# A two-layer mixture-of-experts kernel on one core: first layer's slots split behind three blocks, hidden units on partitions, GpSimd clears ahead of stores

## The chip, the cores and the metric

One Trainium2 chip (trn2), one core. The metric is the device time in microseconds of one launch; the median of 3 runs is 466.99 us (463.61 to 469.23).

## The reference

Shapes: `x` is (32, 128, 128), that is 4096 tokens of 128 values. Two layers, each a residual:

```python
def _L0_cond_ref(x, y, w, coeffs):             # polynomial in side input, condition and x
    X = jnp.stack([jnp.ones_like(x), x, x * x], axis=1)
    ...
    dW = jnp.einsum('abc,kaj,kbi,kcij->kij', coeffs, X, Y, Wp)
def _L0_ffn_ref(x, Wg, bg, W1, b1, W2, b2):     # 8 experts, 2 per token, hidden 256
    logits = jnp.einsum('bsd,de->bse', x, Wg) + bg
    ...
    h = jax.nn.gelu(jnp.einsum('bsd,edh->besh', x, W1) + b1[None, :, None, :], approximate=False)
    out = jnp.einsum('besh,ehd->besd', h, W2) + b2[None, :, None, :]
    y = jnp.einsum('bse,besd->bsd', gates, out)
def _L1_cond_ref(x, h0, Wx, Wh, b):             # recurrence over the 128 positions
    ...
        next_h = jnp.tanh(xp_t + prev_h @ Wh)
def _L1_ffn_ref(...):                           # layer norm, router, shared expert, 8 experts, 2 per token
    out = _swiglu(xf, sWg, sWu, sWd)
    for e in range(NUM_EXPERTS):
        out = out + w[:, e:e + 1] * _swiglu(xf, Wg[e], Wu[e], Wd[e])
x = x + _L0_ffn_ref(_L0_cond_ref(fside_BxS_0, cond_1024, x, L0_cond_coeffs), ...)
x = x + _L1_ffn_ref(_L1_cond_ref(x, cond_1024, L1_cond_Wx, L1_cond_Wh, L1_cond_b), ...)
```

## The kernel before

The program is written by engine: one function for each of SyncE (SP), GpSimd (POOL), ScalarE (ACT), VectorE (DVE) and TensorE (PE), each executed in the order in which it is written, held together by semaphores. The 4096 tokens are cut into 8 blocks of 512 (16 positions of 32 sequences). Each layer sorts its tokens by expert through DRAM: a GpSimd indirect DMA sends the 128 rows of one tile and one choice into `regions` (`send`), SyncE loads 128 rows of one expert back at a time, which is one slot, and after the expert a second indirect DMA (`send_result`) stores the slot's 128 result rows into `results`, in the order of the tokens. 8192 choices need 64 slots, and up to 7 more for the experts' ragged ends: 71 per layer.

Stages, in order of time:

- First part. Blocks in groups (0), (1, 2), (3, 4), (5, 6), (7): transposes, the polynomial, the router (`choose`, `gates`, `positions`). GpSimd runs `scatter0(g)`: 64 sends, each behind `rest()`, a memset of a tile and a wait for it. `copy_z` of a group waits until the group two earlier is sent, since the rows' buffers are a ring of two.
- First layer's slots, `slots0` on PE, ACT and DVE: for slot j the rows are transposed, copied by ACT (`copy_turned0`), multiplied with W1 (`hidden_slot`: tokens on the partitions of the result, 256 columns), DVE adds the bias (`add_bias`), ACT takes the gelu, PE transposes twice (`turn_act`), ACT copies (`copy_act`), PE multiplies with W2 (`slot_down`), DVE adds the bias and multiplies with the gate (`gate_result`), and GpSimd stores. `SLOTS` splits the slots in two parts, each with a table that says which expert and which rows a slot takes: the first part (`FULL_SLOTS`) needs only the sends of the groups up to `CUT`, the second all of them. `DONE` says how many stores must have landed before the blocks up to the cut can be read back (`parts`). The results' ring `y_row` has 24 places, so DVE can be 24 slots ahead of GpSimd.
- Recurrent bodies, `stream_body(i, i % 2)` for i = 0 to 7: the 16 steps of block i, one PE matmul and one ACT tanh each, and between them the work of other blocks, placed by tables of step numbers (`PAIR_AT`, `DOWN_AT`, `LOGIT1_AT`, `XP_AT`, ...): layer norm, router and shared expert of block i - 1, the sum x1 of block i + 1 (`add_one`, `sum_x1`, `turn_back`). GpSimd's part of a body is `inv_std(n)` (the inverse standard deviation that `logits1(n)` on DVE waits for) and `scatter1(m)`.
- Second layer's slots, `slots1`: 4 slots of the last block's shared expert, then 71 of the experts. On GpSimd the eight sends of block 6 stand ahead of the layer's store 0, and the eight of block 7 one each ahead of stores 8 to 15 (`SCATTER_AT`).
- End: `load_parts` reads the results back, `add_parts` sums, the output is written.

GpSimd's program in a row: the factors, `scatter0` of five groups, 71 `send_result(0, r)`, then in a loop `inv_std(i - 1)` and the sends that are due, then 71 `send_result(1, r)`. `inv_std(0)` so stands behind the first layer's last store:

```python
            for r in range(LAYER_SLOTS[0]):
                send_result(0, r)
            m = 0
            for i in range(1, NB):
                inv_std(i - 1)
                while m < SPLIT * NT * TOPK and scatter_step(m) < STEPS * (i + 1) + VAR_STEP:
                    scatter1(m)
                    m += 1
```

In a body DVE works through `positions`, `variance1`, `add_shared`, `sum_x1`, `multiply(i - 1, 0)`, `logits1`, `choose`, `multiply(i - 1, 1)`, `gates`; PE's `down1` of a half c waits for `multiply(i - 1, c)`, and what stands behind `down1` on PE, the next step of the recurrence too, waits with it.

## Time and profile before

| what | us |
|---|---|
| median of 3 runs | 466.99 (463.61 to 469.23) |
| profiled execution, device time | 464.02 |
| its span, first to last instruction | 462.2 |
| TensorE busy, share of the span | 398.0 (86%) |
| VectorE busy | 339.4 (73%) |
| GpSimd busy | 307.9 (67%) |
| ScalarE busy | 206.6 (45%) |

The profiled execution's device time is 1.8 us above its span. A row of the timeline gives start, duration, engine, line, operation, output<-input, count, and in brackets how long the engine had been idle before and what released it. Names are those of the tensors; buffer numbers are left out. "issue" is idle time for which the profile shows no releaser.

### The profile page before, as it was taken

The page shows a single profiled execution, that of the slowest core. Times are in us where ns is not written, and L with a number is a line of the kernel's source. Part 1 is how long each engine was busy: PE and PEld are TensorE (multiplying, and loading weights), DVE is VectorE, ACT ScalarE, POOL GpSimd, SP SyncE. Part 2 cuts the span into 40 slices and gives each one's busy share as a digit, 9 for nine tenths or more (in the row PEclk, how much of TensorE's full clock was granted, in tenths as well). Part 3 has the DMA queues.
Part 4 walks back from the last instruction along what each step waited for, and adds up shares of the span by engine and source line. Part 5 has one row for each costly group of instructions (what it writes and reads, how often), then busy time and mean ns, then how long its engine had stood idle before and what let it go on. Part 6 is the DMA issues. An engine that isn't in the chain of part 4 may idle for free.

```text
span 462.2 us, 10225 instructions
## 1 busy us (share of the span) xinstructions
PE 398.0 (86%) x2428; PEld 324.8 (70%) x2428; DVE 339.4 (73%) x1299; ACT 206.6 (45%) x660; POOL 307.9 (67%) x369
## 2 busy tenths in 40 slices
PE   3888868366999999999999999997985999999950
PEld 3475635354799999976778888775774888888840
DVE  4788885538788888885767776878689566677782
ACT  1121204040677777754554554553442455555520
POOL 0548888888877777777346666665645777676670
PEclk9898785557799999999999999999898899999985
DMA  5996111113454444263311111112421353333756
GB/s 147 276 328 198 41 42 40 40 44 96 111 145 113 106 116 108 78 193 128 109 63 42 42 42 36 41 42 72 105 62 54 87 136 104 99 94 83 276 159 210
DMA packets 48150, 49.79 MB, mean 108 GB/s; under 512 B 8627, under 2 KB 37246, under 8 KB 47966
## 3 DMA queue, kind: packets, MB, share of 16 engines
q1 hardware_dynamic: 38680, 30.46, 24.5%
q0 software_dynamic: 8640, 17.84, 11.6%
q10 hardware_dynamic: 774, 0.84, 0.6%
q8 instruction: 23, 0.38, 0.3%
q14 instruction: 33, 0.27, 0.2%
HBM read 27.99 MB, written 21.12 MB: 106 GB/s over the span
## 4 chain that ended last, share of the span: by engine, by line
PE 60%; DVE 13%; POOL 12%; issue 6%; DMA 5%; ACT 1%; SPq 1%; DVEq 0%; POOLq 0%; ACTq 0%
PE banks L1271 49%; POOL regions L519 9%; PE banks L1275 8%; PE banks L1360 3%; POOL pause L509 3%; DMA parts<-results 3%; DMA results<-y_row,y_dest 1%; DMA base<-in_x 1%; POOL results L553 1%; DVE y_row L1053 1%; DVE act_row L1151 1%; DVE state_lo L1144 1%; DMA regions<-parts,pos 1%; ACT wgu_hi L617 0%; DVE blocks L978 0%
## 5 line engine op out<-in xcount | busy, mean ns | idle before, releaser
L553 POOL DMA_INDIRECT results<-y_row,y_dest x142 | 138.1, 973 | 56.9 <-issue 33.2
L519 POOL DMA_INDIRECT regions<-first_w,pos x64 | 62.9, 983 | 45.9 <-ACT hT L654 30.6
L519 POOL DMA_INDIRECT regions<-parts,pos x64 | 65.0, 1016 | 18.0 <-POOL pause L509 18.0
L654 ACT ACTIVATE hT<-banks,pcol 128x32 f32<-128x32 f32 x128 | 36.9, 288 | 52.9 <-PE banks L1271 52.3
L636 ACT COPY act_col<-banks 128x256 f32<-128x256 f32 x146 | 54.0, 370 | 11.0 <-PE banks L1275 10.1
L713 ACT ACTIVATE silu_row<-banks 128x256 f32<-128x256 f32 x75 | 28.8, 384 | 63.8 <-PE banks L1271 63.1
L1275 PE MATMUL banks<-const_sb,act_row 128*128 128x128 f32 x292 | 56.8, 277 | 0.0
L1271 PEld LDWEIGHTS banks<-hT,wh 128*128 128x128 f32 x256 | 39.2, 188 | 23.3 <-ACT hT L654 19.9
L1275 PEld LDWEIGHTS banks<-const_sb,act_row 128*128 128x128 f32 x292 | 41.7, 143 | 18.3 <-issue 1.8
L1151 DVE TENSOR_TENSOR act_row<-silu_row,banks 128x256 f32<-128x256 f32 x75 | 31.4, 420 | 28.8 <-ACT silu_row L713 26.1
L1271 PE MATMUL banks<-hT,wh 128*128 128x32 f32 x256 | 50.3, 279 | 0.0
L1271 PE MATMUL banks<-first_w,state 128*128 x142 | 44.7, 398 | 1.7 <-DVE silu_row L1038 1.4
L1271 PE MATMUL banks<-wd,act_col 128*128 x284 | 44.4, 280 | 1.0 <-DVE y_row L1053 0.9
L1271 PE MATMUL banks<-first_w,act_col 128*128 x284 | 43.7, 276 | 0.5 <-ACT act_col L636 0.3
L1271 PEld LDWEIGHTS banks<-wd,act_col 128*128 128x128 f32 x284 | 38.0, 195 | 1.4 <-issue 1.3
L1271 PEld LDWEIGHTS banks<-first_w,act_col 128*128 128x128 f32 x284 | 37.3, 191 | 1.2 <-issue 1.2
L1271 PE MATMUL banks<-hT,sw_raw 128*128 128x256 f32 x112 | 38.0, 421 | 0.0
L630 ACT ACTIVATE act_row<-silu_row 128x256 f32<-128x256 f32 x71 | 29.6, 417 | 14.4 <-DVE silu_row L1038 12.0
L1271 PE MATMUL banks<-wgu_hi,state_hi 128*128 x71 | 35.0, 492 | 0.7 <-issue 0.3
L1038 DVE TENSOR_TENSOR silu_row<-banks,first_w 128x256 f32<-128x256 f32 x71 | 29.6, 418 | 5.7 <-issue 3.0
L1271 PE MATMUL banks<-parts,xpow 96*128 96x512 f32 x48 | 30.7, 792 | 0.4 <-DVE parts L790 0.4
L509 POOL MEMSET pause<- 128x256 f32 x80 | 26.0, 326 | 5.6 <-issue 5.5
(192 smaller groups left out, 855.1 us busy)
## 6 DMA issues: line engine op xcount, KB each, us to landing
parts<-results SPq DMA_DIRECT2D x16, 512.0 KB, 5.0
hT<-regions SPq DMA_DIRECT2D x71, 65.0 KB, 2.1
wgu<-regions SPq DMA_DIRECT2D x71, 65.0 KB, 1.9
results<-y_row,y_dest POOLq DMA_INDIRECT x142, 2.3
base<-in_x SPq DMA_DIRECT2D x12, 128.0 KB, 3.1
out<-base SPq DMA_DIRECT2D x20, 64.0 KB
regions<-const_sb SPq DMA_DIRECT2D x18, 65.0 KB
first_w<-in_L_ffn_W SPq DMA_DIRECT2D x1, 1024.0 KB, 8.1
```

Source lines behind the costliest of these rows:

```text
L509: pool.memset(pause[:, :], 0.0).then_inc(rested, 1)
L519: pool.indirect_dma_start(regions[layer], bass.IndirectOffsetOnAxis(ap=poss[layer][q][:, t, k:k + 1], axis=0), hrows[layer][:, q, t, k, :] ...
L553: pool.indirect_dma_start(results[layer], bass.IndirectOffsetOnAxis(ap=y_dest[:, s:s + 1], axis=0), y_row[:, s, :], None).then_inc(results ...
L630: nc.scalar.activation(act_row[:, j % ACT_RING, :], silu_row[:, j % SILU_RING, :], ACT.Gelu).then_inc(slot_act[0], 1)
L636: nc.scalar.copy(act_col[:, j % ACT_RING, :], act_turned_ps[:, j % 2, 0:HID]).then_inc(act_copied[layer], 1)
L654: nc.scalar.activation(hT[:, hcols(n, step_col(s), B)], rnn_ps[:, p, step_col(s):step_col(s) + B], ACT.Tanh, bias=pcol[:, ROW_CB:ROW_CB + ...
L713: nc.scalar.activation(silu_row[:, q % SILU_RING, :], up_ps[:, q % 2, 0:HID], ACT.Silu).then_inc(slot_silu, 1)
L1038: dve.tensor_tensor(silu_row[:, j % SILU_RING, :], up_ps[:, j % 2, 0:HID], b1[:, bass.ds(e * HID, HID)], ALU.add).then_inc(biased, 1)
L1151: dve.tensor_tensor(act_row[:, q % ACT_RING, :], silu_row[:, q % SILU_RING, :], up_ps[:, q % 2, HID:2 * HID], ALU.mult).then_inc(slot_act[ ...
L1271: return nc.tensor.matmul(dst, w, v, start=start, stop=stop, **kw)
L1275: ins = nc.tensor.transpose(bank[:, t * P:(t + 1) * P], tile, ident)
L1360: nc.tensor.transpose(turned_ps[:, r % 2, 0:P], rows[layer][:, s, 0:D], ident).then_inc(turned[layer], 1)
```

## The change

- `CUT` goes from 2 to 1 and the first layer's first part from 32 slots to 16: it needs only the sends of blocks 0 to 2, the other 55 slots all of them. `DONE[0]` so goes from 47 stores to 31.
- The first expert's hidden units stand on the partitions: DVE copies a slot's W1 (128x256) into a ring (`copy_w1`), PE multiplies it, 128 columns at a time, with the transposed rows, ACT applies gelu with the bias from `pcol` by a column chosen in a register. `add_bias`, `turn_act` and `copy_act` are gone from the first layer; the last block's shared slots also lose their transposes and copies. Lags, rings and PSUM buffers are changed to suit.
- `rest()` clears 256 columns of `ypow` (96 partitions) in place of `pause` (128 partitions), and stands ahead of every `send_result` of both layers too. The sends of the bodies have none, as before, and lose a wait for the send before.
- In a body `down1`'s tiles are spread over steps 8, 9, 11, 12 and 14, 15, 15, 15; the ranks of the last blocks go from step 15 to 13; x1 of block 3 is made inside body 2, behind `multiply(1, 0)`.
- GpSimd's factors of block 2 wait for the first group's choice. The second part's table has temporaries of its own. The last sums are made by halves of a block. In body 7 `multiply_slot(0)` and `(1)` stand ahead of `gate_rows`.

```diff
-CUT = 2
-ALL_SLOTS, FULL_SLOTS = TOPK * TOK // P + E - 1, (32, 40)
+CUT = 1
+ALL_SLOTS, FULL_SLOTS = TOPK * TOK // P + E - 1, (16, 40)
...
-AHEAD, ACT_LAG, DOWN_LAG = 3, (3, 2), (5, 4)
-STATE_RING, SILU_RING, ACT_RING = 4, 3, 4
+AHEAD, ACT_LAG, DOWN_LAG = (4, 3), 2, (4, 3)
+STATE_RING, SILU_RING, ACT_RING, WEIGHT_RING, WEIGHTS_AHEAD = (6, 4), 3, (8, 4), 3, 2
+DEPTH = 3
...
-ROWS_AT, COPY_ROWS_AT, RANKS_AT, LAST_RANKS_AT = 0, (1, 2), 1, 15
-PAIR_AT, SILU_AT, DOWN_AT = (((2, 3), (5, 6)), ((8, 9), (11, 12))), (4, 10), ((13, 14), (15, 15))
+ROWS_AT, COPY_ROWS_AT, RANKS_AT, LAST_RANKS_AT = 0, (1, 2), 1, 13
+PAIR_AT, SILU_AT = (((2, 3), (5, 6)), ((8, 9), (11, 12))), (4, 10)
+DOWN_TILE_AT = (8, 9, 11, 12), (14, 15, 15, 15)
...
-SUM_AT = 61, 64, 67
+SUM_FROM = 60
+HALF_SUMS = -(-(ALL_SLOTS - SUM_FROM) // 4) * 4
...
             def rest():
 
                 rests[0] += 1
-                pool.memset(pause[:, :], 0.0).then_inc(rested, 1)
+                pool.memset(ypow[:, :, :], 0.0).then_inc(rested, 1)
                 pool.wait_ge(rested, rests[0])
...
-                if layer and t and n < SPLIT:
-                    pool.wait_ge(scattered[layer][q][k], 16 * sent)
...
             for n in range(1, POOL_FACTORS):
+                if n > 1:
+                    pool.wait_ge(chosen_ready[0], n - 1)
...
             for r in range(LAYER_SLOTS[0]):
+                rest()
                 send_result(0, r)
...
+                rest()
                 send_result(1, r)
...
+            def gelu(j, e):
+
+                act.wait_ge(up_ready[0], j + 1)
+                if j >= ACT_RING[0]:
+                    act.wait_ge(result_ready[0], j - ACT_RING[0] + 1)
+                for c in range(NC):
+                    chunk = slice(c * P, (c + 1) * P)
+                    ins = nc.scalar.activation(act_col[0][:, j % ACT_RING[0], chunk], up_of(j)[:, chunk], ACT.Gelu,
+                                               bias=pcol[:, bass.ds(e * NC + ROW_B1 + c, 1)])
+                ins.then_inc(slot_act[0], 1)
...
+            def copy_w1(j, e):
+
+                if j >= WEIGHT_RING:
+                    dve.wait_ge(up_ready[0], j - WEIGHT_RING + 1)
+                dve.tensor_copy(slot_w1[:, j % WEIGHT_RING, :], w1[:, bass.ds(e * HID, HID)]).then_inc(weight_ready, 1)
...
                 if post:
                     multiply(i - 1, 0)
+                    if i == LATE_ONE_AT:
+                        add_one(i + 1)
+                        sum_x1(i + 1)
...
+            def add_last(n):
+
+                for k, (half, landed) in enumerate(((slice(0, BLK // 2), parts1_in[n]), (slice(BLK // 2, BLK), last_half_in))):
+                    dve.wait_ge(landed, 16)
+                    link(dve.tensor_tensor(base[:, n, half], base[:, n, half], parts[:, n, 0, half], ALU.add))
+                    ins = dve.tensor_tensor(base[:, n, half], base[:, n, half], parts[:, n, 1, half], ALU.add)
...
-            def hidden_slot(j, e):
+            def hidden_slot(j):
+                if j >= DEPTH:
+                    pe.wait_ge(slot_act[0], j - DEPTH + 1)
+                pe.wait_ge(weight_ready, j + 1)
                 pe.wait_ge(state_ready[0], j + 1)
-                if j >= 2:
-                    pe.wait_ge(biased, j - 1)
-                mm(up_ps[:, j % 2, 0:HID], state0[:, j % STATE_RING, :], w1[:, bass.ds(e * HID, HID)]).then_inc(up_ready[0], 1)
+                for c in range(NC):
+                    chunk = slice(c * P, (c + 1) * P)
+                    ins = mm(up_of(j)[:, chunk], slot_w1[:, j % WEIGHT_RING, chunk], state0[:, j % STATE_RING[0], :])
+                ins.then_inc(up_ready[0], 1)
```

GpSimd, from the last send of `scatter0` on, before: the 71 stores stand in a row (L553 is `send_result`, L545 `inv_std`).

```order
L509 MEMSET pause 128x256
L519 DMA regions<-parts,pos 33920x130
L553 DMA results<-y_row,y_dest 17280x128 x71
L545 TENSOR_TENSOR rstd<-var,const_sb 128x4
L519 DMA regions<-first_w,pos 33920x130
```

GpSimd after the change, the end of the same piece (L573 is `send_result`, L532 the memset of `rest`, L565 `inv_std`).

```order
L532 MEMSET ypow 96x256
L573 DMA results0<-y_row,y_dest 17280x128 [waits y_ready0,results_out9,rested]
L532 MEMSET ypow 96x256
L573 DMA results0<-y_row,y_dest 17280x128 [waits y_ready0,results_out10,rested]
L565 TENSOR_TENSOR rstd<-var,const_sb 128x4 [waits var_ready]
```

Ahead of each of the 142 stores a memset has come, and the store waits for it; `inv_std(0)` still stands behind the last store of the first layer.

TensorE in body 4, steps 9, 10 and 13 to 15 before (each step begins with `hT,wh`; `hT,sw_raw` is the shared expert's first product, `sw_raw,first_w` is `down1`, a tile each, `stream,wx` the recurrence's input, `const_sb,base` `turn_back`).

```order
L1271 MATMUL banks<-hT,wh 128x32
L1271 MATMUL banks<-hT,sw_raw 128x256
L1271 MATMUL banks<-hT,wh 128x32
L1275 MATMUL banks<-const_sb,base 128x128 x4
...
L1271 MATMUL banks<-hT,wh 128x32
L1271 MATMUL banks<-sw_raw,first_w 128x128 x2
L1271 MATMUL banks<-stream,wx 128x256
L1271 MATMUL banks<-hT,wh 128x32
L1271 MATMUL banks<-sw_raw,first_w 128x128 x2
L1271 MATMUL banks<-stream,wx 128x256
L1271 MATMUL banks<-hT,wh 128x32
L1271 MATMUL banks<-sw_raw,first_w 128x128 x4
```

And now, from step 12 on (steps 8, 9 and 11 read as 12 does).

```order
L1332 MATMUL banks<-hT,wh 128x32
L1332 MATMUL banks<-hT,sw_raw 128x256
L1332 MATMUL banks<-sw_raw,first_w 128x128
L1332 MATMUL banks<-hT,wh 128x32
L1332 MATMUL banks<-stream,wx 128x256
L1332 MATMUL banks<-hT,wh 128x32
L1332 MATMUL banks<-stream,wx 128x256
L1332 MATMUL banks<-sw_raw,first_w 128x128
L1332 MATMUL banks<-hT,wh 128x32
L1332 MATMUL banks<-sw_raw,first_w 128x128 x3
```

Four of the eight `down1` tiles have moved out of steps 13 and 14 into steps 8, 9, 11 and 12, and one from step 15 to 14.

## Rows read from the trace of the kernel before

**Rows 1.** Stages by stretch: us, PE, PEld, DVE, ACT, POOL busy (instructions), clock, DMA, GB/s

```profile
205.00:306.00 101.00, 101.00 (x637) 79.30 (x638) 73.69 (x327) 52.27 (x160) 61.34 (x62) 1.00 0.20 65
357.00:440.00 83.00, 82.84 (x540) 72.27 (x541) 57.76 (x222) 44.25 (x161) 59.66 (x67) 0.97 0.44 128
```

**Rows 2.** Timeline of GpSimd: last send of the first layer, first store

```profile
130.44 0.33 POOL L509 MEMSET pause<- 128x256 f32 x1
131.04 0.96 POOL L519 DMA_INDIRECT regions<-parts,pos  x1 [0.28 <-POOL pause L509]
132.31 0.98 POOL L553 DMA_INDIRECT results<-y_row,y_dest  x1 [0.30 <-issue]
```

**Rows 3.** Timeline of GpSimd: last first-layer store, inv_std(0)

```profile
221.50 0.96 POOL L553 DMA_INDIRECT results<-y_row,y_dest  x1 [0.30 <-issue]
223.24 1.42 POOL L545 TENSOR_TENSOR rstd<-var,const_sb 128x4 f32<-128x4 f32 x1 [0.78 <-DVE var L838]
```

**Rows 4.** Timeline of PE: one first-layer slot, and the start of the next

```profile
142.34 0.27 PE L1360 MATMUL banks<-const_sb,hT 128*128 128x128 f32 x1
142.45 0.60 PE L1271 MATMUL banks<-first_w,state 128*128 x2
142.88 0.38 PE L1275 MATMUL banks<-const_sb,act_row 128*128 128x128 f32 x2
143.10 0.61 PE L1271 MATMUL banks<-first_w,act_col 128*128 x4
143.54 0.27 PE L1360 MATMUL banks<-const_sb,hT 128*128 128x128 f32 x1
```

**Rows 5.** Body 1, timeline of DVE and ACT: both multiplies, tanh of its step 15, of body 2's step 0

```profile
224.60 0.69 DVE L1093 TENSOR_TENSOR first_w<-first_w,banks 128x512 f32<-128x512 f32 x1 [0.24 <-PE banks L1271]
229.35 0.69 DVE L1093 TENSOR_TENSOR first_w<-first_w,banks 128x512 f32<-128x512 f32 x1
231.72 0.29 ACT L654 ACTIVATE hT<-banks,pcol 128x32 f32<-128x32 f32 x1 [0.81 <-PE banks L1271]
232.84 0.29 ACT L654 ACTIVATE hT<-banks,pcol 128x32 f32<-128x32 f32 x1 [0.83 <-PE banks L1271]
```

**Rows 6.** Timeline of ACT: tanh of steps 12 and 13 of body 4

```profile
269.73 0.29 ACT L654 ACTIVATE hT<-banks,pcol 128x32 f32<-128x32 f32 x1
270.51 0.29 ACT L654 ACTIVATE hT<-banks,pcol 128x32 f32<-128x32 f32 x1 [0.38 <-PE banks L1271]
```

**Rows 7.** Timeline of PE, body 2: step 15 with four tiles of `down1`

```profile
245.28 0.30 PE L1271 MATMUL banks<-hT,wh 128*128 128x32 f32 x2
245.42 1.14 PE L1271 MATMUL banks<-sw_raw,first_w 128*128 128x128 f32 x8
246.40 0.31 PE L1271 MATMUL banks<-hT,wh 128*128 128x32 f32 x2
```

**Rows 8.** Clock after PE's idle 3.5 us in the second slots, columns as in rows 1

```profile
359.00:361.00 2.00, 2.00 (x10) 1.90 (x9) 1.12 (x4) 0.93 (x3) 1.51 (x2) 0.50 0.34 101
363.00:365.00 2.00, 2.00 (x14) 1.69 (x13) 1.28 (x7) 0.82 (x3) 1.44 (x3) 1.00 0.29 87
```

**Rows 9.** Timeline of GpSimd: second layer's stores 10, 45 and 70 (counted from 0)

```profile
360.45 0.95 POOL L553 DMA_INDIRECT results<-y_row,y_dest  x1 [0.30 <-issue]
413.53 0.96 POOL L553 DMA_INDIRECT results<-y_row,y_dest  x1 [0.40 <-issue]
450.17 0.95 POOL L553 DMA_INDIRECT results<-y_row,y_dest  x1 [0.30 <-issue]
```

**Rows 10.** DMA issues by line: count, KB, median us from issue to landing

```profile
results<-y_row,y_dest POOLq DMA_INDIRECT x142, 2.3
```

**Rows 11.** Timeline of DVE: a slowed router operation of the first group

```profile
19.92 1.00 DVE L873 TENSOR_TENSOR rt_score<-rt_score,const_sb 128x32 f32<-128x32 f32 x1
```

**Rows 12.** Groups of instructions, DVE in the first layer's slots: busy us, mean ns | idle before

```profile
L1038 DVE TENSOR_TENSOR silu_row<-banks,first_w 128x256 f32<-128x256 f32 x71 | 29.6, 418 | 5.7 <-issue 3.0 <-PE banks L1271 2.4
L1053 DVE TENSOR_SCALAR y_row<-y_row,hT 128x128 f32<-128x128 f32 x71 | 22.0, 310 | 0.0
```

More of the change, by code:

```diff
@@ L421, in load_parts @@
             def load_parts(n):
-                sp.dma_start(parts[:, n, :, :], result_rows[1][n]).then_inc(parts1_in[n], 16)
+                if n < NB - 1:
+                    sp.dma_start(parts[:, n, :, :], result_rows[1][n]).then_inc(parts1_in[n], 16)
+                else:
+                    for half, landed in ((slice(0, BLK // 2), parts1_in[n]), (slice(BLK // 2, BLK), last_half_in)):
+                        sp.dma_start(parts[:, n, :, half], result_rows[1][n][:, :, half]).then_inc(landed, 16)
             def load_weights():
@@ L638, in slots0, with copy_act @@
+            def copy_act(q):
+                act.wait_ge(act_turned, q - SHARED_SLOTS + 1)
+                if q >= ACT_RING[1]:
+                    act.wait_ge(result_ready[1], q - ACT_RING[1] + 1)
+                nc.scalar.copy(act_col[1][:, q % ACT_RING[1], :], act_turned_ps[:, q % 2, 0:HID]).then_inc(act_copied, 1)
             def slots0():
-                lag, count = ACT_LAG[0], LAYER_SLOTS[0]
-                for j in range(AHEAD):
+                count = LAYER_SLOTS[0]
+                for j in range(AHEAD[0]):
@@ L649, in slots0 @@
+                load_tables(ACT.Silu)
                 copy_x1(0)
-                copy_act(0, count - 1)
             def tanh_step(n, p, s):
@@ L715, in slots1 @@
             def slots1():
[L716 removed]
+                last, lag, count = NB - 1, ACT_LAG, SHARED_SLOTS + LAYER_SLOTS[1]
                 for k in range(TOPK):
@@ L758, in _ @@
             slots0()
-            load_tables(ACT.Silu)
             act.wait_ge(y_ready[0], HELD_ROWS)
@@ L1047, in gate_result @@
                 row, y = rows[layer][:, r % ROWS_RING, :], y_row[:, s, :]
-                gate, result = row[:, D:D + 1], result_ps[:, q % 2, 0:D]
+                gate, result = row[:, D:D + 1], result_of(layer, q)
                 if layer == 0:
@@ L1055, in slots0 @@
             def slots0():
-                lag = DOWN_LAG[0]
-                experts = []
-                for j in range(LAYER_SLOTS[0]):
-                    if j % READ == 0:
-                        d = int(j >= SLOTS[0])
-                        experts = [*experts[-lag:], *table_values(dve, d, j - FIRST_SLOT[d], READ, E - 1)]
-                    k = j % READ + min(j - j % READ, lag)
-                    add_bias(j, experts[k])
+                lag, count, experts = DOWN_LAG[0], LAYER_SLOTS[0], {}
+                for j in range(-WEIGHTS_AHEAD, count + lag):
+                    w = j + WEIGHTS_AHEAD
+                    if w < count:
+                        if w % READ == 0:
+                            d = int(w >= SLOTS[0])
+                            experts.update(enumerate(table_values(dve, d, w - FIRST_SLOT[d], READ, E - 1), w))
+                        copy_w1(w, experts[w])
                     if j == 1:
@@ L1114, in stream_body @@
                     add_one(n)
-                if ahead:
+                if ahead and i != LATE_ONE_AT:
                     sum_x1(i + 1)
@@ L1125, in stream_body @@
                         make_table(2)
-                    gates(1, i - 1, (i - 1) % 3)
+                    if ahead:
+                        gates(1, i - 1, (i - 1) % 3)
+                    else:
+                        gate_values(1, i - 1)
+                        multiply_slot(0)
+                        multiply_slot(1)
+                        gate_rows(1, i - 1, (i - 1) % 3)
                 for n in ONE_AT[1].get(i, ()):
@@ L1436, in slots1 @@
                     r = q - SHARED_SLOTS
+                    if r >= 0:
+                        for row in rows_at(q):
+                            turn_rows(1, row)
                     if q == POST_AT["ranks"]:
@@ L1439, in slots1 @@
                         ranks1(last)
-                    if r >= 0:
-                        for row in rows_at(q):
-                            turn_rows(1, row)
                     if r < 0:
@@ L1564, in stream_body @@
                             rnn_input(i + 1, 1 - p, XP_AT.index(s))
+                    if post:
+                        for c in range(NC):
+                            tiles = [t for t in range(NT) if DOWN_TILE_AT[c][t] == s]
+                            if tiles:
+                                down1(i - 1, 1 - p, c, tiles)
                     if i >= SPLIT and s == LAST_RANKS_AT:
```

222 lines of the change are left out of this document (117 added, 105 removed).

## The prediction

> **What bounds the kernel now.** I read the stages by stretch first, then GpSimd's timeline from end to end, then PE's, DVE's and ACT's timelines at the places where the chain of waits changes engine. The stretches show PE busy nearly throughout in the bodies (205 to 306 us) and the second slots (357 to 440) [rows 1]. GpSimd is less busy on average, but its timeline shows where it leads. It goes from its last send straight to its first store, at 132.31, so the sends set where the stores begin [rows 2]. From there 71 stores run to 221.50, one every (221.50 - 132.31) / 70 = 1.274 us, and `inv_std(0)`, for which body 1 waits, follows at 223.24 and ends at 224.66 [rows 3]. It waited 0.78 us for DVE there, so today GpSimd's queue is just not late: it has under 1 us in hand. At the end it leads again: store 70 starts at 450.17 and the program ends at 462.2, 12.0 us later, with the store's landing, the last loads, sums and output behind it [rows 9].
>
> **GpSimd's clears.** A send with its memset takes 0.33 + 0.28 + 0.96 = 1.57 us; from the last send to the first store, without one, it is 132.31 - 131.04 = 1.27 [rows 2]. So a clear ahead of a store costs 0.30 us of GpSimd's own time. Nothing overlaps: the memset starts when the operation before it ends, and the store waits for it. 96 partitions in place of 128 I price the same; bounds 0.25 to 0.33. This is paid 142 times, and counts wherever GpSimd is never idle.
>
> First layer: the sends end as before, but for the first group. There DVE's router operations take 1.00 us while GpSimd works on the factors of block 2 [rows 11]; with two such operations moved clear of it, and some of the contention coming back in `condition(1)`, I take 0.7 us earlier (0 to 1.5). First store at 132.31 + 0.30 - 0.7 = 131.9, then 70 x (1.274 + 0.305) = 110.5: store 70 starts at 242.4 and ends at 243.4. With 0.2 us of gap and 1.42 for `inv_std(0)` [rows 3] the deviation is there at 245.0, where it was 224.66.
>
> Who waits: in body 1 DVE's `logits1(0)`, behind it on DVE `choose` and `multiply(0, 1)`. ACT waits for the choice at step 12, PE for the product at step 14, the recurrence behind both. From the first multiply's end (225.29), when the deviation was there, to the second's end (230.04) it is 4.75 us of chained small operations [rows 5]. So the product comes at 249.75, tanh 15 about 0.6 us later at 250.35, and body 2's first tanh 0.89 later at 251.2. Before, it was at 232.84 [rows 5]: **18.4 us later**. After such a stop PE comes back at the lower of its clock's two levels, 1.2 instead of 2.4 GHz: behind a stop of some 3.5 us that ended at 357, the granted clock was 0.50 from 359 to 361 and 1.00 from 363 [rows 8]. If that lasts for 4 to 6 us, at most half of it is lost, and only in steps that PE limits: 0 to 2.8 us, and I take **2.0**.
>
> Second layer: stores 45 to 70 come every 36.64 / 25 = 1.47 us, at PE's pace [rows 9]; with the clear GpSimd needs 1.567 and never catches up. The place from which it runs without a gap is store 10, behind DVE's making of the last table; with the results one slot earlier (`DOWN_LAG` 4 to 3) this is about 357.4 in the old kernel's time instead of 360.45 [rows 9]. From there 5 sends and 60 stores at 1.567 are 101.9, plus 0.7 for a few long ones as before: store 70 at 460.0 against 450.17, **9.8 us later**. The results' ring of 24 doesn't stop DVE: store 46 lands some 35 us before result 70 is due.
>
> **The first slots.** On PE a slot takes 0.11 for the rows' transpose, 0.43 for the hidden product, 0.22 for two transposes and 0.44 for the second product, 1.20 in all [rows 4]. The new hidden product has twice the instructions with half the columns, 0.44. So 0.98, which is 71 x 0.22 = 15.6 us off PE. ACT loses a copy of 0.37 and splits the gelu, and DVE exchanges `add_bias` (0.418 [rows 12]) for a copy of 256 columns, for which I allow 0.17 to 0.42. No engine gets slower, and all of it lies beside GpSimd's stores. None of the 15.6 us arrives. The sends still end at 131, and slot 16 now needs all of them: with the 2.3 us of a landing [rows 10] its rows can be loaded from about 133.6 and are there near 137, while PE waits ahead of slot 12 (12 slots from 117 at 1.0). Then 59 slots at 1.05 would end near 200. But result 70 needs store 46 landed: 131.9 + 46 x 1.579 + 2.3 = 206.8 [rows 2, 10]. Body 0 so starts about 2 us later than today's 205, far ahead of the stop in body 1, which swallows that. Reading the parts after 31 stores (181 us) rather than 47 (194) is early for the same nothing. Block 3's parts need all stores, near 245, and are used in body 2: no further wait.
>
> **The bodies.** Steps that follow the recurrence alone take 0.78 us [rows 6]; step 15 takes 1.12, for its own product needs 0.14 and four tiles of `down1` 0.98, that is 0.245 each [rows 5, 7]. Steps 13 and 14, with two tiles and a half of the recurrence's input (256 columns, 0.43 by rows 4), come to 1.06 and more; I take three steps at 1.10, 0.95 us over per body. Spread out, a step with a pair or an input and one tile needs 0.14 + 0.43 + 0.25 = 0.82, on five steps, and step 15 with three tiles 0.88: 0.28 over. Gain 0.67 a body. Body 1's is lost in the stop, bodies 2 to 5 give 2.7, and body 6, whose ranks also leave step 15, 0.9: **3.6 us**. With the first two shared slots multiplied earlier I take **0.6** more (0 to 1.2) where the second slots begin.
>
> **End.** Behind the last landing two sums of 512 columns (0.69 each, by rows 5) become two of 256 (0.418, by rows 12): 0.54 less, of which I take **0.4**, for one more load is issued.
>
> **Sum.** 18.4 + 2.0 + 9.8 - 3.6 - 0.6 - 0.4 = 25.6 us over the profiled execution's 464.0: 489.6. That execution was 3.0 under the median of 467.0, so the median lies between 489.6 and 492.6, and I say 491.
>
> **A rule against this.** The stores take 0.96 us in the first layer, where DVE's `y_row` operation reads SBUF alone (0.310 us each [rows 12]), and 0.95 to 0.96 in the second, where it reads PSUM [rows 2, 3, 9]. So no lock shows. The Trainium skill (SBUF - State Buffer, Who interferes with whom) says that an fp32 copy from SBUF to SBUF on VectorE can take the port shared with GpSimd for the whole instruction, so that GpSimd cannot write descriptors; `copy_w1` is such a copy. By that rule the rival with the lock below would hold, by these rows it would not.
>
> **Rivals.**
> - *The clears are free* (0.04), the one on the faster side. The place is GpSimd's queue between stores; if the memset hid in the 0.30 us gap, the pace would stay 1.27, and below about 1.29 nothing waits in body 1. Then bodies give 0.68 x 5 + 0.9 = 4.3, the change of stage 0.6, and the earlier results with the end about 3: 456 profiled, 459. For it: the gap is marked "issue" with no owner. Against it: the sends have exactly this form and take 1.57.
> - *A lock by the weight copies* (0.07). DVE's 71 copies hold up descriptor writing. Each is up to 0.42 us long by the nearest row; at half of that, 71 x 0.21 = 15 us are added ahead of `inv_std(0)`: 506.
> - *Only one of the two places pays* (0.15). The last stores could start from an earlier anchor, or PE's stop be partly used by other work: without the second layer's 9.8 but for 2, 483; without the clock's 2.0 as well, 481. For it: in the second layer the pace differs by only 0.1 us from PE's. Against it: 8 more sends with their clears come in the same queue.
> - *Nothing much changes* (0.03): gains of PE and clears cancel. It needs the 20 us in body 1 to vanish, which no row supports.
>
> The forecast has 0.71.
>
> **Range and chances.** The forecast's own bounds are 484 to 498 (clear 0.25 to 0.33, clock 0 to 2.8, the two anchors 1.5 each). Taking in the rival with one place paid, 479 to 500. This kernel's measurement tells about 1% from no change: faster 0.04, within 1% 0.03, slower 0.93.
>
> **What would show it.** Store to store 1.57 to 1.58 us in the first slots, `inv_std(0)` near 244, tanh idle 15 us or more in body 1, a clock of 0.50 behind it, steps 13 to 15 of the bodies at 0.80 to 0.90, and stores of the second layer at 1.57 without idle to the end. PE idle near 128 to 137. It is wrong if stores come every 1.27, if body 1 runs through, or if GpSimd waits for DVE late in the second slots.

## The result, and the profile after

The changed kernel took 500.21 us (median of 4 runs, 495.48 to 501.78) where the kernel before took 465.77 (4 runs, 463.61 to 469.23): ratio 1.072 [1.061, 1.082], 7% slower. The forecast was 491 (479 to 500). The experiments below add what no row of before could show: on a second chip, where the kernel before takes 541 us, the same change is 6% faster. This section is about the first chip; that these runs were made on the chip of the first experiments follows from the kernel before alone, 465.8 us here and 466.1 there. A run over 1.5% above the fastest of its kernel is left out throughout, and of kernel b below that leaves only one, of 481.3 us, for the other took 490.8.

The profiled executions were 464.0 before and 495.5 after, 31.5 us apart; the sum had 25.6.

| | before | after | later by |
|---|---|---|---|
| first store of layer 0 (GpSimd) | 132.31 | 131.84 | -0.5 |
| its store 70 | 221.50 | 245.32 | 23.8 |
| first tanh of body 0 | 206.65 | 209.99 | 3.3 |
| first tanh of body 2 | 232.84 | 254.88 | 22.0 |
| last tanh of body 7 | 313.39 | 334.22 | 20.8 |
| layer 1's store 0 | 335.72 | 354.64 | 18.9 |
| its store 10 | 360.45 | 378.36 | 17.9 |
| its store 70 | 450.17 | 481.88 | 31.7 |
| end of the span | 462.2 | 493.7 | 31.5 |

Read downwards, the last column gives the mechanism: it rises at two places, both in rows of GpSimd's stores, and comes back by 4 us in between.

Groups of instructions, GpSimd after:

```profile
L573 POOL DMA_INDIRECT results<-y_row,y_dest x142 | 139.6, 983 | 43.7 <-POOL ypow L532 31.6 <-DVE y_row L1082 9.8 <-issue 2.3
L532 POOL MEMSET ypow<- 96x256 f32 x222 | 73.4, 331 | 3.7 <-issue 3.5
```

142 of the 222 clears are new. Timeline of GpSimd after, at the first store [rows 2], in the first slots, and at the end of the stores [rows 3]:

```profile
130.27 0.96 POOL L539 DMA_INDIRECT regions<-parts,pos  x1 [0.28 <-POOL ypow L532]
131.24 0.33 POOL L532 MEMSET ypow<- 96x256 f32 x1
131.84 0.97 POOL L573 DMA_INDIRECT results<-y_row,y_dest  x1 [0.28 <-POOL ypow L532]
133.41 0.97 POOL L573 DMA_INDIRECT results<-y_row,y_dest  x1 [0.28 <-POOL ypow L532]
...
141.26 0.97 POOL L573 DMA_INDIRECT results<-y_row,y_dest  x1 [0.28 <-DVE y_row L1082]
142.23 0.40 POOL L532 MEMSET ypow<- 96x256 f32 x1
142.92 0.96 POOL L573 DMA_INDIRECT results<-y_row,y_dest  x1 [0.28 <-POOL ypow L532]
...
208.90 1.46 POOL L573 DMA_INDIRECT results<-y_row,y_dest  x1 [0.28 <-POOL ypow L532]
210.35 0.33 POOL L532 MEMSET ypow<- 96x256 f32 x1
211.84 1.06 POOL L573 DMA_INDIRECT results<-y_row,y_dest  x1 [1.16 <-issue]
...
245.32 0.96 POOL L573 DMA_INDIRECT results<-y_row,y_dest  x1 [0.28 <-POOL ypow L532]
246.31 1.04 POOL L565 TENSOR_TENSOR rstd<-var,const_sb 128x4 f32<-128x4 f32 x1
```

Store to store is 1.57 us, and 1.65 or 1.66 where the memset takes 0.40 instead of 0.33; eleven memsets of the first slots do. The store at 202.17 takes 1.42 us, the one at 208.90 1.46, and those from 211.84 to 215.30 1.06 to 1.21; all of these stand beside operations of DVE on 512 columns (the sums of x1 and `wgu_lo`). So the mean pace is (245.32 - 131.84) / 70 = 1.621. The deviation stands behind the last store and is ready at 247.35, where it was 224.66.

Timeline of DVE and of ACT after, in body 1: the first operation that needs the deviation, the second multiply, and the tanh of steps 12 to 15 and of body 2's step 0 [rows 5]:

```profile
247.38 0.19 DVE L876 TENSOR_TENSOR rt_logit<-banks,rstd 128x32 f32<-128x32 f32 x1 [18.32 <-POOL rstd L565]
251.33 0.69 DVE L1120 TENSOR_TENSOR first_w<-first_w,banks 128x512 f32<-128x512 f32 x1
```

```profile
232.78 0.29 ACT L685 ACTIVATE hT<-banks,pcol 128x32 f32<-128x32 f32 x1
...
249.54 0.27 ACT L685 ACTIVATE hT<-banks,pcol 128x32 f32<-128x32 f32 x1
250.53 0.29 ACT L685 ACTIVATE hT<-banks,pcol 128x32 f32<-128x32 f32 x1 [0.73 <-PE banks L1332]
253.17 0.29 ACT L685 ACTIVATE hT<-banks,pcol 128x32 f32<-128x32 f32 x1 [2.35 <-PE banks L1332]
254.88 0.29 ACT L685 ACTIVATE hT<-banks,pcol 128x32 f32<-128x32 f32 x1 [1.42 <-PE banks L1332]
```

The recurrence stands still for 16.76 us, and its next steps take 0.99, 2.64 and 1.71 us. The windows behind the stop, and the bodies' stretch [rows 1, 8] (columns as in rows 1):

```profile
205.00:306.00 101.00, 83.45 (x503) 67.56 (x502) 58.12 (x247) 40.62 (x126) 67.62 (x86) 0.89 0.20 63
```

```profile
240.00:250.00 10.00, 0.14 (x1) 0.14 (x1) 2.24 (x12) 0.41 (x2) 6.21 (x10) 0.50 0.19 55
252.00:254.00 2.00, 1.93 (x9) 1.93 (x10) 1.62 (x12) 0.29 (x1) 0.00 (x0) 0.50 0.67 205
256.00:258.00 2.00, 2.00 (x14) 1.55 (x12) 1.05 (x7) 1.61 (x5) 0.00 (x0) 1.00 0.81 249
```

PE worked 101.00 of 101 us in this stretch before, and 83.45 now. Its granted clock is 0.50 (1.2 GHz) from the stop until 254 and 1.00 from 256.

Timeline of PE after, ahead of slot 12: its rows need every send.

```profile
127.81 0.61 PE L1332 MATMUL banks<-first_w,middle 128*128 x4
134.66 0.47 PE L1421 MATMUL banks<-const_sb,hT 128*128 128x128 f32 x1 [6.24 <-DMA hT<-regions]
```

### The profile page after: what moved, and what is told of

Same layout as the page of the kernel before. It is cut to its first block and busy times, and to the rows that moved or that the text cites. A ratio compares the mean times of both kernels' runs of the same rounds, so it can differ in the third digit from the quotient of the medians.

```text
span 493.7 us, 10269 instructions
## 1 busy us (share of the span) xinstructions
PE 389.8 (79%) x2444; PEld 328.4 (67%) x2444; DVE 331.2 (67%) x1307; ACT 196.9 (40%) x656; POOL 355.7 (72%) x511
## 5 line engine op out<-in xcount | busy, mean ns | idle before, releaser
L573 POOL DMA_INDIRECT results<-y_row,y_dest x142 | 139.6, 983 | 43.7 <-POOL ypow L532 31.6
L532 POOL MEMSET ypow<- 96x256 f32 x222 | 73.4, 331 | 3.7 <-issue 3.5
L657 ACT ACTIVATE middle<-banks,pcol 128x128 f32<-128x128 f32 x142 | 44.6, 364 | 26.4 <-PE banks L1332 25.8
L1332 PE MATMUL banks<-state,slot_w 128*128 128x128 f32 x284 | 46.7, 289 | 8.1 <-DVE slot_w L1067 3.8
L1189 DVE TENSOR_TENSOR middle<-middle,banks 128x256 f32<-128x256 f32 x75 | 31.4, 420 | 26.7 <-ACT middle L744 25.2
L1332 PEld LDWEIGHTS banks<-state,slot_w 128*128 128x128 f32 x284 | 40.0, 204 | 9.5 <-DVE slot_w L1067 3.9
L1332 PE MATMUL banks<-first_w,middle 128*128 x284 | 44.7, 282 | 2.0 <-DVE y_row L1082 2.0
L1332 PE MATMUL banks<-wd,middle 128*128 x284 | 44.4, 280 | 0.1
L1332 PE MATMUL banks<-hT,sw_raw 128*128 128x256 f32 (+1 forms) x144 | 42.0, 389 | 0.5 <-DVE middle L1189 0.5
L1332 PEld LDWEIGHTS banks<-first_w,middle 128*128 128x128 f32 x284 | 38.6, 198 | 2.4 <-issue 2.4
L1332 PEld LDWEIGHTS banks<-wd,middle 128*128 128x128 f32 x284 | 38.3, 196 | 0.5 <-issue 0.5
```

The lines of the kernel that those rows point to most:

```text
L532: pool.memset(ypow[:, :, :], 0.0).then_inc(rested, 1)
L573: pool.indirect_dma_start(results[layer], bass.IndirectOffsetOnAxis(ap=y_dest[:, s:s + 1], axis=0), y_row[:, s, :], None).then_inc(results ...
L657: ins = nc.scalar.activation(act_col[0][:, j % ACT_RING[0], chunk], up_of(j)[:, chunk], ACT.Gelu, bias=pcol[:, bass.ds(e * NC + ROW_B1 + c ...
L1189: dve.tensor_tensor(into[:, q % ACT_RING[1], :], silu_row[:, q % SILU_RING, :], up_ps[:, q % 2, HID:2 * HID], ALU.mult).then_inc(slot_act[ ...
L1332: return nc.tensor.matmul(dst, w, v, start=start, stop=stop, **kw)
```

## The experiments

Four jobs; within each, all kernels and the kernel before ran on one chip. The results name the chip of the first job as 0 (the kernel before took 466.1 us there) and that of the other three as 10 (546.7, 541.0 and 540.3). A ratio is to the kernel before in the same job.

| kernel | clears ahead of | median us | ratio |
|---|---|---|---|
| first job, before at 466.1 | | | |
| a, change without clears ahead of stores | sends | 457.9 | 0.983 [0.976, 0.989] |
| c, clears ahead of layer 1's stores only | sends, layer 1 | 470.9 | 1.012 [1.003, 1.020] |
| b, clears ahead of layer 0's stores only | sends, layer 0 | 481.3 | 1.033 (one run, no interval) |
| d, before, with its clear ahead of all stores | all | 502.7 | 1.080 [1.071, 1.089] |
| second job, before at 546.7 | | | |
| e, change with no clear anywhere | none | 561.0 | 1.024 [1.013, 1.035] |
| g, as a, `CUT` back to 2 | sends | 550.7 | 1.011 [1.004, 1.017] |
| h, change, all clears of 128 columns | all, half | 538.6 | 0.988 [0.980, 0.996] |
| f, change, deviation ahead of store 62 | all | 510.5 | 0.936 [0.929, 0.944] |
| third job, before at 541.0 | | | |
| i, the change itself | all | 509.3 | 0.943 [0.935, 0.950] |
| j, f again | all | 500.5 | 0.926 [0.920, 0.932] |
| fourth job, before at 540.3 | | | |
| k, d again | all | 504.4 | 0.941 [0.929, 0.954] |
| l, change, three one-column clears for each | all, tiny | 533.6 | 0.992 [0.987, 0.998] |

### Where the time goes on the first chip: a, b, c, d

a takes both lines out, b the one of layer 1, c the one of layer 0; in d they are added to the kernel before.

```diff
             for r in range(LAYER_SLOTS[0]):
-                rest()
                 send_result(0, r)
...
-                rest()
                 send_result(1, r)
```

> The changed kernel without the clears ahead of the 142 stores; the sends keep theirs. Queue theory (GpSimd's added 0.30 us a store, in body 1 and at the end, is the whole loss): stores every 1.27 us, store 70 of the first layer near 222, inv_std(0) near 224, no stop in body 1, steps 8 to 15 of the bodies at 0.78 to 0.89 us, second slots at PE's 1.47 us; 457 to 462 us. Rival A (the weight copies on VectorE hold up GpSimd): stores still lengthened in the first slots, body 1 still stops for several us; 468 or more. Rival B (the new split or the new slots make the loss): 480 or more.

> The changed kernel with clears ahead of the first layer's stores only. Queue theory: the stop in body 1 stays (step 12 some 16.8 us), body 2's first tanh near 255, second slots at PE's 1.47 us; the second layer's share of some 10 us is gone: 483 to 488 us. A theory in which the two costs are one (the later one only shows what is left of the first): within 3 us of the changed kernel or within 3 us of the one without clears.

> The changed kernel with clears ahead of the second layer's stores only. Queue theory: no stop in body 1, body 2's first tanh near 233, stores of the second layer every 1.57 us without idle from about store 10; 468 to 474 us. If the end's loss depended on the late start of the layer: under 463 us.

> The kernel before with a clear (its own, 128 partitions by 256 columns) ahead of each of the 142 stores and nothing else. Queue theory: body 1 stops, inv_std(0) 20 to 22 us later, last stores 10 us later still than the bodies' shift; 494 to 502 us, slightly above the changed kernel, whose bodies and tail are shorter. Rival B (clears harmless, the split or slots at fault): under 475 us.

a and c came where the queue theory had them, d 0.7 us above its range of 494 to 502, and b's one run 1.7 below its range of 483 to 488; none came near a rival. Against a, layer 0's clears cost 23.4 us (b) and layer 1's 13.0 (c), together 36.4, and the changed kernel stands 42.3 above a. By the profiled executions it is 20.8 and 10.0, together 30.7, against 34.9. So the two costs are separate, and make up most of the loss; with one run of b, and 6 us between the runs of the changed kernel, whether anything is left over isn't shown. Timeline of GpSimd, the end of layer 0's stores, in a:

```profile
220.41 0.96 POOL L573 DMA_INDIRECT results<-y_row,y_dest  x1 [0.30 <-issue]
221.67 0.96 POOL L573 DMA_INDIRECT results<-y_row,y_dest  x1 [0.30 <-issue]
222.65 1.05 POOL L565 TENSOR_TENSOR rstd<-var,const_sb 128x4 f32<-128x4 f32 x1
```

and in b, which has this layer's clears alone:

```profile
243.90 0.96 POOL L573 DMA_INDIRECT results<-y_row,y_dest  x1 [0.28 <-POOL ypow L532]
244.86 0.33 POOL L532 MEMSET ypow<- 96x256 f32 x1
245.46 0.96 POOL L573 DMA_INDIRECT results<-y_row,y_dest  x1 [0.28 <-POOL ypow L532]
246.45 1.04 POOL L565 TENSOR_TENSOR rstd<-var,const_sb 128x4 f32<-128x4 f32 x1
```

In b body 1 stops for 17.06 us as in the changed kernel. In a no step of body 1 takes over 2.5 us, and body 2 begins at 229.98. d has the stop too, of 9.54 us, shorter since its body 1 arrives later: its body 0 begins at 217.02. So neither the new split nor the weight copies are needed for the loss.

a is the change's other half by itself, and beats the kernel before by 8.2 us. With all clears present (500.2 for the changed kernel against 502.7 for d, not in one job) 2.5 us are left of it.

### The second chip: e, f, g, h

e takes out the clears of the sends as well as those of the stores:

```diff
                     for k in range(TOPK):
-                        rest()
                         send(0, g, t, k)
...
-                        rest()
                         scatter1(SPLIT * NT * TOPK + i)
...
-                rest()
                 send_result(1, r)
```

g is a with the old cut:

```diff
-CUT = 1
-ALL_SLOTS, FULL_SLOTS = TOPK * TOK // P + E - 1, (16, 40)
+CUT = 2
+ALL_SLOTS, FULL_SLOTS = TOPK * TOK // P + E - 1, (32, 40)
...
-LATE_ONE_AT = GROUPS[CUT][-1]
+LATE_ONE_AT = 2
```

h clears 128 columns, f keeps 256 and has the deviation earlier:

```diff
-                pool.memset(ypow[:, :, :], 0.0).then_inc(rested, 1)
+                pool.memset(ypow[:, 0, :], 0.0).then_inc(rested, 1)
```

```diff
             for r in range(LAYER_SLOTS[0]):
                 rest()
+                if r == 62:
+                    inv_std(0)
                 send_result(0, r)
...
-                inv_std(i - 1)
+                if i > 1:
+                    inv_std(i - 1)
```

> The changed kernel with no clear anywhere: the 64 sends of the first layer and 16 of the second lose theirs too. Queue theory: sends every 1.27 us instead of 1.57, the first store 64 x 0.30 = 19 us earlier, near 113; the first slots then start when the router of the last group is through, some 10 us earlier; 440 to 450 us. Rival: the clears protect the sends from something (a full ring, long landings), sends get longer by as much as they save: 455 us or more.

> The changed kernel, all clears kept, with inv_std(0) ahead of GpSimd's store 62 of the first layer instead of behind store 70. Queue theory: the deviation is there near 234 instead of 247, body 1's stop shrinks from 16 to about 3 us, and the next wait is block 3's parts, which need all 71 stores (landed near 250, loaded near 254): body 2 stops for 2 to 5 us; 488 to 494 us. If the stop in body 1 had another cause than this wait: no change from 500.

> The changed kernel without the clears ahead of stores, and with the split undone (first part 32 slots behind blocks 0 to 4; x1 of block 3 still late). PE's wait of 6 us ahead of slot 12 goes, but GpSimd's stores start at the same time, and inv_std(0) stands behind the last of them: within 1.5 us of the kernel without store clears, 456 to 460 us. If PE's wait were on the path: 450 to 453.

> The changed kernel with every clear cut from 256 to 128 columns. A clear should take about 0.19 us instead of 0.33, so a store 1.43 instead of 1.57 us. Queue theory: the first layer's loss of 28 us against the kernel without store clears falls by 71 x 0.14 = 10 us, and the sends give 64 x 0.14 = 9; in the second layer 1.43 is under PE's 1.47, so that loss nearly goes, 13 to 3: 467 to 474 us. If each clear cost a fixed time whatever its size: 498 to 502.

All four times missed what the queue theory gave, since it assumed a kernel before at 466. (e's rival, 455 us or more, has the number, but not for its reason: the sends of the first layer did not get longer, 1.01 us on average against 1.02 in a.) And the times stand in the opposite order: the fewer clears, and the smaller, the slower. The theory that a clear only costs its own time fell here.

The page of e says where to look. Its GpSimd is busy for 51% of the span, where a's is for 67%, and the chain that ended last has a share that no page of the first chip has (first line by engine, of e, the second of a):

```profile
PE 54%; DVE 21%; another core or an unknown queue 11%; issue 8%; ACT 2%; DMA 2%; DVEq 1%; SPq 0%; POOLq 0%; ACTq 0%; POOL 0%
```

```profile
PE 38%; DVE 8%; issue 2%; POOL 2%; DMA 1%; POOLq 1%; ACT 0%; DVEq 0%; SPq 0%; ACTq 0%
```

Timeline of e in the first slots, PE, GpSimd, ACT and DVE:

```profile
148.54 0.61 PE L1328 MATMUL banks<-first_w,middle 128*128 x4
148.99 0.27 PE L1417 MATMUL banks<-const_sb,hT 128*128 128x128 f32 x1
...
150.55 0.61 PE L1328 MATMUL banks<-first_w,middle 128*128 x4
150.78 0.96 POOL L572 DMA_INDIRECT results<-y_row,y_dest  x1 [0.31 <-issue]
...
152.82 0.27 ACT L644 COPY state<-banks 128x128 f32<-128x128 f32 x1 [2.97 <-remote]
152.91 0.29 DVE L1075 TENSOR_TENSOR y_row<-banks,first_w 128x128 f32<-128x128 f32 x1 [3.37 <-remote]
...
153.87 0.96 POOL L572 DMA_INDIRECT results<-y_row,y_dest  x1 [2.12 <-DVE y_row L1078]
```

The copy at 152.82 is ACT's copy 16 of the layer, and the transpose that it reads, PE's number 16, was done near 149.3 (148.99 + 0.27). DVE's operation at 152.91 is its number 7 and needs product 7, which began at 148.54 and was done near 149.2. By these rows ACT and DVE stood still together for 3 us behind results that were there, and PE and then GpSimd ran out of work behind them. e's first store, expected near 113, came at 141.50. After 120 us e has 19 stretches over 0.6 us in which PE, ACT and DVE are all idle; those in the first slots last 0.8 to 2.1 us and come mostly some 7 or 14 us apart. Counted in stores, it is every fourth: in e the stores that come over 2 us behind the one before are 3, 7, 11, 15, 20, 24, 28, 32, 36, 40, 44 and 48 (counted from 0) and four more, and in g and h they are mostly four apart too. a has two such stretches in all, at PE's wait for slot 12's rows and at the end. In one stretch of both, 140 to 180 us, e and then a (columns as in rows 1):

```profile
140.00:180.00 40.00, 31.05 (x234) 29.56 (x233) 19.70 (x96) 18.89 (x74) 21.75 (x23) 0.91 0.33 84
```

```profile
140.00:180.00 40.00, 40.00 (x361) 40.00 (x360) 35.10 (x161) 31.65 (x121) 30.55 (x32) 1.00 0.47 125
```

e lets 23 stores through, a 32. A single store takes 0.96 us in both, so nothing is slow in itself: the engines are kept waiting. In f, with all clears, only 3 joint stretches are left.

What they wait for is a signal from PE. In this program an engine tells the others that a result is there by adding one to a semaphore, and the trace records when an increment happened (some are missing). Between 125 us and 3 us before the end, every increment in all six traces of the first chip is recorded within 0.04 us of the end of its instruction. On the second chip the same holds for DVE, ACT and GpSimd, but in each of the eight traces some 180 to 220 of PE's 510 to 620 come over 0.3 us late. Around the stop shown, seven increments of PE, whose instructions ended from 149.15 to 151.16, are all recorded between 152.76 and 153.07.

### Is it the clears, or the split of the slots? i, j, k, l

i is the changed kernel unedited, j is f, k is d. l:

```diff
-                pool.memset(ypow[:, :, :], 0.0).then_inc(rested, 1)
+                pool.memset(ypow[:, 0, 0:1], 0.0)
+                pool.memset(ypow[:, 0, 1:2], 0.0)
+                pool.memset(ypow[:, 0, 2:3], 0.0).then_inc(rested, 1)
```

> The changed kernel itself, beside the kernel before, to see whether the verdict holds wherever it runs. On the chip of the last four runs the kernel before took 546.7 us instead of 466, and in the traces of kernels with few clears PE, ACT and DVE stood still together for 1 to 2 us every 7 to 14 us while GpSimd's stores followed each other at 1.27 us; with 256-column clears (pace 1.57) they did not. Theory 1 (the clears keep the engines from standing still, on a chip that shows this; elsewhere they only cost GpSimd time): if the kernel before takes about 466 us here, this one takes 495 to 505 (ratio 1.06 to 1.08); if it takes about 546, this one takes 518 to 535 (ratio 0.95 to 0.98), what f took and most of the 17 us stop of body 1. Theory 2 (that chip is slower at everything, and f was fast there for its earlier deviation alone): the ratio stays at 1.06 to 1.08 wherever it runs, 580 to 590 us if the kernel before takes 546.

> All clears kept, the first chain's deviation computed on GpSimd ahead of store 62 instead of behind store 70. If the kernel before takes about 466 us here: queue theory (the stop of 16.8 us in body 1 is the deviation's place behind the stores, and no other thing of the first layer costs on the way) 483 to 490, 12 to 17 us below the changed kernel, since the second layer's stores remain at 1.57 us; rival (the stores themselves, or the results' reload behind them, hold the body) no more than 5 us below it. If the kernel before takes about 546: 509 to 513, as before, and 9 to 22 us below the changed kernel.

> The kernel before with its own clear ahead of all 142 stores, and nothing else of the change. Where the kernel before takes about 466 us: 502 (ratio 1.08), as measured. Where it takes about 541: theory 1 (the clears are what makes the changed kernel faster there, the split of the slots adds little) 508 to 520, ratio 0.94 to 0.96, at most 8 us behind the changed kernel's 509; rival (on that chip the new order of the slots and the partitions brings the gain) 535 or more, or slower than the kernel before.

> The changed kernel with each 256-column clear replaced by three of one column (about 0.10 us each by the small memsets of the profile, so stores stay some 1.57 to 1.65 us apart while almost nothing is written). Theory of the pace (the other engines stand still where GpSimd's indirect transfers follow each other too closely, and the clear only keeps them apart): within 1% of the changed kernel, 505 to 515 where the kernel before takes about 541, 495 to 503 where it takes 466. Theory of the work (what the clear itself does on its engine matters, so columns count): on the chip where the kernel before takes 541 this one takes 530 to 560, with joint pauses of PE, ACT and DVE of 1 to 2 us back in the trace; where it takes 466, no difference from the changed kernel beyond the pace.

i came out at 0.943: theory 1, and faster than it said (509 against 518 to 535). Theory 2, a chip slower at everything, would have given 580 or more. k has the clears without the rest of the change and comes to 0.941, where its rival needed 535 or more. So on this chip the clears bring the whole gain, about 36 us (this kernel takes nearly the same on both chips, 502.7 in d and 504.4 in k), and the split, the partitions and the bodies add nothing that these runs can tell. Stretch 140 to 180 of i, beside e's above:

```profile
140.00:180.00 40.00, 36.04 (x287) 33.67 (x287) 26.65 (x124) 24.54 (x94) 33.04 (x51) 0.97 0.39 99
```

j is 8.7 us below i, just short of the 9 to 22 expected (f, the same kernel, is at 0.936 of its kernel before where i is at 0.943, so the gain may be as little as 4 us): the deviation runs at 233.05 instead of 247.49, body 1 runs through where i stops for 8.25, and body 2 then stops for 6.60 behind its step 10. That the stop on the first chip is the deviation's place in GpSimd's queue fits this, but j or f never ran there.

l did not keep the pace that it was to keep. The three memsets overlap, as its timeline of GpSimd shows:

```profile
155.66 0.96 POOL L575 DMA_INDIRECT results<-y_row,y_dest  x1 [0.28 <-issue]
156.62 0.11 POOL L532 MEMSET ypow<- 96x1 f32 x1
156.65 0.12 POOL L533 MEMSET ypow<- 96x1 f32 x1
156.67 0.12 POOL L534 MEMSET ypow<- 96x1 f32 x1
157.08 0.96 POOL L575 DMA_INDIRECT results<-y_row,y_dest  x1 [0.28 <-issue]
```

Stores so come every 1.42 us and not every 1.57, and the pauses are back (12 joint stretches). The time fell where the theory of the work had it, but its premise, equal pace, was not met. Put by the usual gap between undisturbed stores of layer 0, the kernels of this chip nearly line up (the last column is by how much PE's late increments are late, in us, median):

| | gap us | stores of layer 0 over 2 us apart | median us | late by |
|---|---|---|---|---|
| e, g (no clear ahead of stores) | 1.27 | 16, 15 | 561, 551 | 1.45, 1.34 |
| l (3 x 1 column) | 1.42 | 12 | 534 | 1.11 |
| h (128 columns) | 1.47 | 11 | 539 | 1.11 |
| i, k (256 columns) | 1.57 | 2, 1 | 509, 504 | 0.74, 0.90 |

l clears 3 columns and h 128, yet they are about equal, which with the times of arrival speaks for the pace and against the columns; that l, with the shorter gap, is the faster of the two doesn't fit a pace alone. A delay of the same length without a clear would settle it and wasn't tried, so that it is the pace is argued, not shown. Whether it is the chip itself or a condition it was in during all three jobs isn't shown either: they agree within 1.2% on the kernel before, but lie within a quarter of an hour, and the kernel before has no trace from there.

## Why the prediction was right, and where it was not

Right, for the chip on which the kernel before takes 466:

- **Clears on GpSimd's own time.** 1.57 us from send to store and from store to store, by [rows 2]; first store 131.84 against 131.9 forecast. a to d show that the clears alone make the loss. The rival "the clears are free" gave 459 for a kernel whose stores keep their 1.27 us pace, and a, which has exactly that, took 457.9.
- **Body 1.** The stop is at step 12, on `logits1(0)`, the product is there 4.67 us after the deviation (251.33 + 0.69 - 247.35; forecast 4.75 by [rows 5]), and the clock of 0.50 behind it lasts until 254 to 256. First tanh of body 2: 22.0 us later, forecast 20.4.
- **PE ahead of slot 12** idles 6.24 us, and nothing of the first slots' 15.6 us arrives.
- **The second layer's stores** run from store 10 to 70 without idle but for one gap of 1.19 us, at 431.05.

Mis-sized terms, in the order of the sum:

- *The clock and body 1, 20.4.* It was 22.0. The pace of the first stores was taken as 1.579 and was 1.621, so store 70 started at 245.32 and not 242.4. Over 70 x 1.57 these are 3.6 us: up to 195 us the long memsets and a few longer stores make 1.2, the store at 202.17 makes 0.5, and long stores and a gap from 208.90 to 217 make 1.9. The deviation took 0.6 less (1.04 us and no gap), and the clock cost 1.4 and not 2.0: tanh 15 came 1.15 us behind the product instead of 0.6, the next 1.71 behind that instead of 0.89. The first store was on time for a reason that failed: the sends did not start 0.7 us earlier (28.85 against 28.90), yet the last was 0.8 earlier.
- *The bodies, -3.6.* Between body 2's first tanh and body 7's last only 1.2 us came back. A step with a pair or an input and one tile takes 0.88 us and not 0.82, five times a body. Steps 13 to 15 took 1.10, 1.10 and 1.12, and are 0.78, 0.88 and 0.89; steps 8, 9, 11 and 12 rose from 0.78 to 0.88. That is 0.77 gained and 0.40 lost, 0.4 a body and not 0.67. Body 2's step 14 takes 1.23 us and not 0.88, for block 3's x1 stands ahead of the product on DVE, which the sum left out. Body 6 gave 0.5 and not 0.9, since its step 13 now takes 1.32, and body 7, where the sum had nothing, lost 0.4 by the tiles in its steps 8 to 12.
- *Change of stage, -0.6.* It was -1.9: 20.8 later at the last tanh, 18.9 at layer 1's first store.
- *Second layer, +9.8.* It was 12.8 (18.9 at store 0, 31.7 at store 70), and the runs c and a differ by 13.0. The anchor failed: store 10 was to come 3.0 us earlier by itself, for results one slot earlier, and came 1.0 earlier (17.9). The pace was 1.593 over the 65 transfers and not 1.578.
- *End, -0.4.* It was -0.2.

1.6 + 2.4 - 1.3 + 3.0 + 0.2 are the 5.9 us between 25.6 and 31.5. The median lies 4.7 above the profiled execution and not 0 to 3, so it stands at the range's upper edge, 0.2 above the 500 as written and 2.2 above the forecast's own bound of 498.

**The rule against this.** Most stores kept 0.96 to 0.97 us in the first slots beside `copy_w1`, so the rival with the lock did not happen, and the experiments never need it. Where the Trainium skill (SBUF - State Buffer, Who interferes with whom) has such a copy lock GpSimd out for the whole instruction, the trace shows memsets of 0.40 us instead of 0.33 and one store of 1.11 (at 149.31). "No lock shows" was too wide all the same: beside DVE's operations on 512 columns stores took up to 1.46 us here, and one took 1.26 (at 201.88) in the kernel before.

**What no step contained.** The forecast priced a clear as pure cost and its chance of "faster" was 0.04, by rows of one chip. On the second chip the sign is the other one. The trace of before could not show this: it has no wait for anything unnamed. But it did show a kernel that pays 0.30 us ahead of every send for an instruction whose data nobody reads. That line called for a question, what goes wrong without it, and a rival with a price; the prediction had neither.

## What to carry to other kernels

An instruction that only takes time in front of a queue's transfers costs its own length times the count wherever that queue leads, and what stands behind the row (here one small operation that a recurrence waits for) pays the whole sum: move that out of the row first. Before such a delay is removed or added everywhere, measure on more than one chip, always beside the unchanged kernel: here the same 142 clears in the kernel before add 36.6 us on one (d) and take off 36 on the other (k). And look where a delay's gap falls before taking it for waste: on the second chip signals of another engine pass in it. The fastest version on the first chip is a (457.9), on the second j (500.5); the changed kernel is within 2% of the same time on both (500 and 509), where the kernel before is 16% apart.

## What the runs showed of the hardware that was not expected

- On the second chip, with GpSimd's indirect transfers 1.27 to 1.47 us apart, ACT and DVE stop together for up to 3 us behind results that are there, mostly at every fourth store; at 1.57 us apart the joint stops are nearly gone (2 stores of i over 2 us apart, 16 of e). On the first chip the same 1.27 us run undisturbed for 71 stores.
- The stops are late semaphore increments of PE, and of PE alone: on the second chip some 180 to 220 a trace are over 0.3 us late, by a median of 1.45 us in e and 0.74 in i, and they come in bursts (seven within 0.31 us), in k 186 of 204 of them 1.2 to 1.6 us behind the start of an indirect transfer. On the first chip no increment of any engine is over 0.04 us late between 125 us and the end.
- GpSimd's memsets of one column overlap: starts 0.03 us apart at 0.12 us each. Three are over in 0.17 us, not 0.35, and set the next store back by 0.15 (1.42 us against 1.27).
- A 256-column memset takes 0.33 us, and 0.40 or 0.41 in eleven cases of the first slots, where DVE's weight copies and `y_row` operations run beside it; which of them does this wasn't tried. An indirect transfer of 0.96 us takes up to 1.46 beside DVE's operations on 512 columns.
